# The coded adjacency of a graph kernel: 32 TensorE transposes per row tile against one DMA transpose

## The reference

```
# layer 0: mean over at most 64 neighbours
keep = (A > 0) & (cumsum(A > 0, axis=1) <= 64)
cnt = keep.sum(axis=1)
nb_mean = (keep @ X) / max(cnt, 1)
x = layernorm(x + leaky(X @ W_line.T + b_line) + where(cnt > 0, leaky(nb_mean @ W_nb.T + b_nb), 0))
# layer 1: graph attention over all neighbours
Wh = h @ W + bW
e = leaky(Wh @ a1 + b1 + (Wh @ a2 + b2).T);  e = where(adj > 0, e, -9e15)
x = layernorm(x + softmax(e, axis=1) @ Wh)
```

## Time and profile before

| | before |
|---|---|
| Time, median of 3 runs | 1684.17 us (1682.73 to 1685.88) |
| Span of the profiled execution | 1687.5 us |
| PE busy | 1539.6 us (91%) |
| DVE busy | 1461.6 us (87%) |
| ACT busy | 1056.1 us (63%) |
| DMA queue of SP, share of the 16 engines | 29.1% |
| HBM | 130.29 MB read, 58.72 MB written |

### The profile page before, as it was taken

One profiled execution on the slowest core, in us unless ns is written; L12 is line 12 of the kernel. 1 busy time (PEld: TensorE's weight loads), 2 busy tenths in 40 slices (PEclk: granted clock), 3 DMA queues, 4 the chain that ended last, 5 costly groups with the idle time before them and its releaser, 6 DMA issues. The chain is left out here.

```text
span 1687.5 us, 31015 instructions
## 1 busy us (share of the span) xinstructions
PE 1539.6 (91%) x11552; PEld 951.6 (56%) x11552; DVE 1461.6 (87%) x1687; ACT 1056.1 (63%) x1521; POOL 141.8 (8%) x117
## 2 busy tenths in 40 slices
PE   3999969989899998989899799999999999999996
PEld 2444435555455555555556467676767676766764
DVE  4787889999999999999994598989898989989682
ACT  5733426655555555555554566787777777787873
POOL 0101000111111111111110000000000000000000
PEclk8999979999999999999999899999999999999998
DMA  5521225555455455555542311121221212121101
GB/s 205 193 76 49 76 88 181 175 173 176 162 181 172 169 168 169 172 170 172 169 155 88 106 50 64 38 101 52 76 77 60 89 42 102 51 102 50 39 26 50
DMA packets 81683, 190.51 MB, mean 113 GB/s; under 512 B 7472, under 2 KB 40240, under 8 KB 73392
## 3 DMA queue, kind: packets, MB, share of 16 engines
q1 hardware_dynamic: 74560, 164.91, 29.1%
q0 software_dynamic: 7024, 24.12, 3.7%
HBM read 130.29 MB, written 58.72 MB: 112 GB/s over the span
## 5 line engine op out<-in xcount | busy, mean ns | idle before, releaser
L883 PE MATMUL psum<-reg_ab,reg_c 128*128 128x512 f16 x2048 | 474.1, 389 | 0.0
L1289 PE MATMUL psum<-reg_ab 128*128 128x385 f16 x1024 | 336.2, 328 | 22.7 <-issue 15.0
L1291 PE MATMUL psum<-reg_ab 128*128 128x385 f16 x1024 | 335.7, 328 | 0.0
L1290 PE MATMUL psum<-reg_ab 128*128 128x384 f16 x1024 | 335.4, 328 | 0.0
L883 PEld LDWEIGHTS psum<-reg_ab,reg_c 128*128 128x128 f16 x2048 | 200.9, 100 | 231.2 <-issue 21.8
L1029 ACT ACTIVATE reg_ab<-reg_ab,reg_c 128x512 f32<-128x512 f32 x256 | 170.2, 712 | 114.8 <-DVE reg_ab L1157 114.6
L1157 DVE TENSOR_TENSOR reg_ab<-reg_ab 128x1024 f32<-128x1024 f32 x128 | 156.3, 1222 | 36.3 <-ACT reg_ab L1021 36.3
L1303 PE MATMUL psum<-reg_ab 128*128 128x128 f16 x1024 | 178.5, 219 | 0.0
L1302 PE MATMUL psum<-reg_ab 128*128 128x128 f16 x1024 | 178.5, 218 | 0.0
L1304 PE MATMUL psum<-reg_ab 128*128 128x128 f16 x1024 | 178.4, 218 | 0.0
L639 PE MATMUL psum<-reg_ab 128*128 128x512 f16 x768 | 177.0, 389 | 0.3 <-ACT reg_ab L428 0.3
(11 more groups left out here) (152 smaller groups left out, 2147.3 us busy)
## 6 DMA issues: line engine op xcount, KB each, us to landing
reg_c<-in_adj SPq DMA_DIRECT2D x64, 1024.0 KB, 5.4
m_scratch<-reg_c SPq DMA_DIRECT2D x64, 256.0 KB, 2.3
wt_scratch<-reg_c SPq DMA_DIRECT2D x128, 128.0 KB, 1.8
reg_ab<-wt_scratch SPq DMA_DIRECT2D x32, 512.0 KB, 3.4
reg_c<-m_scratch SPq DMA_DIRECT2D x28, 512.0 KB, 4.7
r_scratch<-reg_ab POOLq DMA_DIRECT2D x32, 256.0 KB, 2.3
r_in<-r_scratch SPq DMA_DIRECT2D x32, 256.0 KB, 2.7
hb_scratch<-xx POOLq DMA_DIRECT2D x32, 256.0 KB, 4.2
```

Source lines behind the costliest of these rows:

```text
L883: last = nc.tensor.matmul(bank[u][:, :], keepT[u][:, j * P:(j + 1) * P], y_parts[:, j, part, :], start=(j == 0 and part == 0), stop=(j == ...
L1289: nc.tensor.matmul(bank[k][:, 0:D + 1 - P], h, v_rows[:, j, P:D + 1], start=(g == 0 and jj == 0), stop=False, skip_group_check=True)
L1290: nc.tensor.matmul(bank[k][:, 0:D - P], h, v_low[:, j, P:D], start=False, stop=False, skip_group_check=True)
L1291: last = nc.tensor.matmul(bank[k][:, 0:D + 1 - P], l, v_rows[:, j, P:D + 1], start=False, stop=end, skip_group_check=True)
```

## The change

TensorE no longer turns the code, and no turned code stands in PSUM. SP issues one DMA transpose per row tile, v_mask (128 x 4096 f16) to keepT viewed as 32 blocks, on two semaphores `turned`. ACT copies each quarter of keepT into the weight code first, and then applies the relu to it in place, waiting for its own copy between the two.

```
-                dve.wait_ge(mask_transposed, 4 * (t - 2) + 2 * s + 2)
+                dve.wait_ge(turned[u], 8 * (t - u))
...
+                def turn_mask(t, u):
+                    sp.wait_ge(v_ready, 2 * t + 2)
+                    if not early(t, 2):
+                        sp.wait_ge(sum_done, t - 1)
+                    sp.sem_inc(wait_done, 1)
+                    sp.dma_start_transpose(keepT[u].rearrange("p (j i) -> p j i", i=P), v_mask[u][:, :]).then_inc(turned[u], 16)
...
                 def step(t, u, prev=True, mask=True, nxt=True, main=True):
+                    if nxt:
+                        turn_mask(t + 1, 1 - u)
                     if main:
                         load_r(t)
...
+                turn_mask(0, 0)
                 for q in range(NQ):
                     store_wt(0, q)
                 run_steps(sp, step)
...
                 def evacuate(t, u, q):
-                    act.wait_ge(mask_transposed, 4 * t + q + 1)
-                    if not early(t, 2) and q == 0:
-                        act.wait_ge(sum_done, t - 1)
-                    src = bank[2 + q % 2][:, :].bitcast(F16)
-                    nc.scalar.activation(keepT[u][:, q * Q * P:(q + 1) * Q * P], src, ACT.Relu, bias=consts[:, 0:1]).then_inc(keep_ready, 1)
+                    if q == 0:
+                        act.wait_ge(turned[u], 8 * (t - u) + 16)
+                    src = keepT[u][:, q * Q * P:(q + 1) * Q * P]
                     if not (early(t, 1) and q < 2):
                         act.wait_ge(wt_stored[q % 2], 16 * (2 * t + q // 2))
                     nc.scalar.activation(wt_q[q % 2], src, ACT.Copy, scale=0.4).then_inc(wt_ready, 1)
+                    act.wait_ge(wt_ready, 4 * t + q + 1)
+                    nc.scalar.activation(src, src, ACT.Relu, bias=consts[:, 0:1]).then_inc(keep_ready, 1)
...
             def _(pe):
-                def transpose_mask(t, u, q):
-                    pe.wait_ge(v_ready, 2 * t + q // 2 + 1)
...
-                    for j in range(Q):
-                        last = nc.tensor.transpose(dst[:, j * P:(j + 1) * P], v_mask[u][:, (q * Q + j) * P:(q * Q + j + 1) * P], ident16[:, :])
...
-                    if nxt:
-                        transpose_mask(t + 1, v, 0)
-                        transpose_mask(t + 1, v, 1)
...
-                    if nxt:
-                        transpose_mask(t + 1, v, 2)
...
-                    if nxt:
-                        transpose_mask(t + 1, v, 3)
```

More of the change, by code:

```diff
@@ L219, in gnn_kernel @@
         cnt_ready, rcp_ready, rc_ready = sem("cnt_ready"), sem("rcp_ready"), sem("rc_ready")
-        mask_transposed, keep_ready, wt_ready = sem("mask_transposed"), sem("keep_ready"), sem("wt_ready")
+        turned = [sem(f"turned{i}") for i in range(2)]
+        keep_ready, wt_ready = sem("keep_ready"), sem("wt_ready")
         wt_stored = [sem(f"wt_stored{i}") for i in range(2)]
@@ L719, in _ @@
                     sp.wait_ge(m_stored[s], 16 * T)
-                sp.wait_ge(mask_transposed, 4 * T)
+                for u in range(2):
+                    sp.wait_ge(turned[u], 8 * T)
                 sp.dma_start(m_first, m_dram[0:CT].rearrange("k p n -> p k n")).then_inc(mfirst_landed, 16)
@@ L865, in _ @@
             def _(pe):
-                def transpose_mask(t, u, q):
-                    pe.wait_ge(v_ready, 2 * t + q // 2 + 1)
-                    if not (early(t, 1) and q < 2):
-                        pe.wait_ge(wt_ready, 4 * t + q - 1)
-                    dst = bank[2 + q % 2][:, :].bitcast(F16)
-                    for j in range(Q):
-                        last = nc.tensor.transpose(dst[:, j * P:(j + 1) * P], v_mask[u][:, (q * Q + j) * P:(q * Q + j + 1) * P], ident16[:, :])
-                        if j == Q - 1:
-                            last.then_inc(mask_transposed, 1)
-                    return last
                 def sums(t, u, q):
@@ L939, in step @@
                         last.then_inc(v_done, 1)
-                    if nxt:
-                        transpose_mask(t + 1, v, 3)
-                for q in range(NQ):
-                    transpose_mask(0, 0, q)
                 run_steps(pe, step)
```

## The result

The changed kernel takes 1704.09 us (median of 4 runs, 1699.29 to 1704.40) against 1683.74 for the kernel before (4 runs): a ratio of 1.0098, 95% interval 1.0072 to 1.0124. It is slower by 20 us where the sum had said 8, and it lies outside the range of 1688 to 1698 us that the prediction gave for its own mechanism, though inside the wide range of 1683 to 1829. The profiled span is 1702.3 us, 14.8 above that of before.

The account below looks back on a forecast made before the run. DVE was taken as the bound; head + 8.8, steady steps 0 and end - 1.0 gave + 7.8 us on 1684.2, so 1692 us. Its own range was 1688 to 1698, the wide one 1683 to 1829.

Parts of the forecast that it names:

- the sum: Whole kernel: head + 8.8, looped and written-out steps 0, end - 1.0, together + 7.8 us.
- The bound: Second block, steady steps: DVE sets the pace, busy 520.26 of 540 us; PE waits about 2 us a step for it.
- PE's wait for L832 grown from 2.0 to over 4 us a step: Steady steps: a sign expected if the forecast held, PE waiting longer for DVE after losing 2.3 us of transposes.
- The head: Start of second block: DVE waits 8.8 us once, as the transposes of tiles 0 and 1 land late.
- D, the time of the transpose: DMA engines' time for the transpose's 1 MB beyond the fixed landing part: taken as 4.1 us, between 2.7 and 10.8.
- The 32 blocks: Rival for the DMA transpose: each 128 x 128 block completes by itself, 58 us a tile, about 3200 us; chance 0.04.
- its loop through SP: Steady steps, issue to next issue of the transpose: 16.65 + D, 20.75 us against 21.37; costs from D = 4.7.
- signs of being wrong: Steady steps: landing over 9.5 us, transpose not overlapping the adjacency load in the queue, or adjacency loads slowed.
- The chain after landing: Steady steps, from the transpose's landing through ACT and PE to SP's next issue: 11.8 us.
- The steady steps at zero: Second block: 24 looped and 5 written-out steps cost 0 us, the new path reaching DVE in time.
- the loop through SP becomes the bound: Rival, steady steps: D from 4.7 to 9 makes SP's order set the pace, 1698 to 1829 us; chance 0.28.
- The end: Last steps of the second block, where DVE isn't the bound: fewer PE transposes give back 1.0 us.

Follow-up runs that it names:

- e2: Changed kernel with each later tile's DMA transpose issued ahead of the last adjacency load, not behind it; 1672.15 us, ratio 0.9919.
- e4: Changed kernel with tile 0's transpose first in the second block and every later one ahead of the last adjacency load; 1663.47 us, ratio 0.9871.
- e3: Changed kernel with tile 0's transpose issued first in the second block, ahead of the flag store and adjacency load; 1693.48 us, ratio 1.0040.
- e1: Changed kernel with 32 unused identity transposes on PE in each step, ahead of its wait for hT; 1686.08 us, ratio 1.0004.
- e5: Kernel before the change with 64 unused identity transposes at the start of PE's program; 1664.64 us, ratio 0.9877.
- e7: Changed kernel with 84 unused identity transposes at the start of PE's program; 1728.70 us, one run.
- e8: Changed kernel with 340 unused identity transposes at the start of PE's program; 1730.96 us, one run.
- e9: The e4 kernel with POOL's bias addition made to wait for DVE's flags of tile t+3's second half; 1663.08 us, ratio 0.9859.

## Why the prediction was right in direction and short in size

**The bound: right.** DVE set the pace, and PE's 2.3 us less a step became waiting. In the stretch from 340 to 880 us PE waits 99 us where it waited 51.2. But the prediction had all of it ahead of the transposed rows ("PE's wait for L832 grown from 2.0 to over 4 us a step"), and the trace has it in two parts: that wait fell to 34.7 us, 1.5 a step, and 64.3 us, 2.7 a step, arose ahead of the product L932. e2 and e4 show steady steps of 21.28 us against 21.37, so taking the transposes from PE brings 0.1 us a step at most.

**The head: right.** Forecast 8.8 us, measured 9.2 in DVE's wait, 9.3 in the account, and e3 takes it away. The landings of tiles 0 and 1 were forecast at about 9.0 and 5.4 us and were 9.6 and 5.6.

**D, the time of the transpose: right in kind, a little low.** Alone it lands in 5.6 us, 4.3 beyond the fixed 1.3, where the prediction took 4.1 from a range of 2.7 to 10.8. By that a 256 byte row costs at most 4.3 x 16 / 4096 = 17 ns, an estimate, far nearer its share of bytes (10.5) than a 1 KB packet (42). The 32 blocks are not completed one by one either: one instruction lands all of them in 5.6 us. The 4.0 us estimated from the Trainium skill ("DMA: Bandwidth & Descriptors", section "Latency and other measured facts") holds within 0.3 us. Behind the adjacency load it lands in 9.6 us (the middle of 24) instead of 8.95, and the adjacency loads in 6.1 instead of 5.4: the two hinder each other, which the sum had left out. In the prediction's own terms that is D = 9.6 - 4.85 = 4.75, just where its loop through SP begins to cost. A landing of over 9.5 us and slower adjacency loads were two of its signs of being wrong, and both are there.

**The chain after landing: right while PE's clock holds.** Forecast 11.8 us to the next issue; from 665.7 to 677.45 it is 11.75. With the landing of 9.5 that makes 21.3 us, a loop without room, and steps of 21.29 to 21.65 us, with one of 22.03, are what the loop has where L932 takes 2.80 us.

**The steady steps at zero: the step that failed.** "+ 0 (24 looped steps) + 0 (5 written out)" was 19.9 for the loop and about 10 for the others, 29.8 together. The prediction said that PE would wait longer and saw no price in it. It priced L937 in the chain at 2.94 us, the value from a trace in which PE came to it straight from its sums. hT now came 5 us later in the step: L793 began 9.0 us after L813 (661.76 - 652.75), L804 begins 14.1 after L824 (647.06 - 633.00); the prediction had 3. So PE waited before that product, the granted clock fell to 0.54, and the product, on the chain with no room left (0.6 us by the prediction's own count), took 4.47. e1 shows it: same landing, PE busy, 13.7 of the 19.9 us gone. The other 6.2 us are not a price of the landing in every step: 5.1 of them are the first looped step. Why the clock holds in every second step, after the same waits, is open.

The rival that fits the time best is *the loop through SP becomes the bound* (1698 to 1829, chance 0.28): 1704 is in its range, and the transpose leaves 3.9 us after its code is ready. It had D as the cause, though, and D alone would have made the loop 16.65 + 4.75 = 21.4 us, level with the 21.37 of before. It was the slow product in the loop that made it 23.

**The end: right.** 1.2 us for 1.0.

**What no step had.** The third block gave back 19.3 us because the removed instructions moved PE's loop. e5, e7 and e8 take the waits away and bring them back by code that does nothing, so the place is the cause, though the rule behind it is open. Where the third block runs alike, the change costs 39.5 us, five times the sum of 7.8. That 1704 came out within 12 us of the forecast 1692 is luck: an error of some 30 us in the second block against a gain of 19 in the third that the prediction knew nothing of.

## What to carry to other kernels

Where an engine is freed but stays in a chain, ask what its new idle time stands in front of: here PE's clock fell after waits, in every second step, and the fall cost time only where the next work was on the path. Put a DMA that someone waits for ahead of a bulk load in the same queue, and look at the head of a block on its own, where the steady cover is missing (moving the calls of the transpose in SP's order took 41 us off). Before a difference of about 1% is put down to an edit, compare the blocks that it doesn't touch: code that did nothing changed a loop here by 3 us and more an iteration.

## What the runs showed of the hardware

- A DMA transpose of 128 x 4096 f16 within SBUF: 5.6 us to landing alone, 9.6 us (the middle of 24) behind a 1 MB load, and 12.5 us once (e1); it moves 4096 packets under 512 B and holds SP's queue for 4.1 us alone and 7.4 us behind the load.
- PE's granted clock fell from 1.00 to 0.54 after waits of 1.5 and 2.6 us with 4.1 us of work between, and 24 products then took 4.47 us for 2.80. In the next step, after waits of 1.5 and 2.6 us again, they took 2.80. After one wait of 4.2 us (e2) 16 sums took 5.72 us for 3.62.
- A PE loop of some 1600 instructions waited 2.7 to 3.5 us in each iteration, marked as issue, where its closing branch lay at remainder 120 or 121 over 256 instructions, and not at 17, 80, 209 or 248 (a unit of 512 fits these runs as well). With it went 79 to 81 instruction packets for 33 to 36.
- DVE and POOL slow each other when they run side by side: DVE's flags 2.23 us for 1.23, its count 5.60 for 4.48, its code 3.18 for 2.29, and POOL's addition 3.17 for 1.26; moving the addition only moves the loss (e9).
